# Slots stage of a fused transformer kernel: a second bank for turned context, weighing as a step's first work, softmax sums one step later with the product on Pool, other places for the layers

## The reference, cut to what matters

```
x_in = _ln(x, lnkv_g, lnkv_b);  k = x_in @ wk + bk;  v = x_in @ wv + bv
slots = q_mu + exp(q_logsig) * noise
for _ in range(3):
    prev = slots
    q = _ln(slots, lnq_g, lnq_b) @ wq + bq
    logits = einsum('bnd,bkd->bnk', k, q) / scale
    attn = softmax(logits, axis=-1) + 1e-8          # over the slots
    attn = attn / sum(attn, axis=1)                 # over the context rows
    upd = einsum('bnk,bnd->bkd', attn, v)
    slots = upd @ wu + bu + prev
    slots = gelu(_ln(slots, lnm_g, lnm_b) @ w1 + b1) @ w2 + b2 + slots
    slots = _ln(slots + x_cls[:, None, :], lnp_g, lnp_b)
```

## Time and profile before

| | us |
|---|---|
| median of 3 runs | 6898.41 (6891.54 to 6907.52) |
| profiled execution | 6899.85 |
| its span | 6897.9 |
| PE busy in the span | 6279.5 (91%) |
| starts of the first and the last score matmul (L3057) | 6233.5 and 6695.3 |
| POOL in the stage's steps | one instruction of 1.89 per step |

### The profile page before, as it was taken

One profiled execution on the slowest core, in us unless ns is written; L12 is line 12 of the kernel. 1 busy time (PEld: TensorE's weight loads), 2 busy tenths in 40 slices (PEclk: granted clock), 3 DMA queues, 4 the chain that ended last, 5 costly groups with the idle time before them and its releaser, 6 DMA issues.

```text
span 6897.9 us, 141178 instructions
## 1 busy us (share of the span) xinstructions
PE 6279.5 (91%) x56181; PEld 4521.0 (66%) x56181; DVE 3982.3 (58%) x8765; ACT 3322.4 (48%) x6373; POOL 2177.0 (32%) x2131
## 2 busy tenths in 40 slices
PE   5799999999999999999978899999699999998988
PEld 4466666666666666666645778777377777747873
DVE  2677777777777777777754244444444444354553
ACT  1466656656666566565643244444233333324543
POOL 3555555545555555555500000000011111082110
PEclk7899999999999999999987899999799999998778
DMA  1565656656656566565711000010100000030000
GB/s 45 90 106 88 105 91 101 107 87 99 100 94 105 89 100 105 87 101 97 114 37 29 19 25 30 28 36 10 34 10 13 11 14 14 18 99 1 1 1 22
DMA packets 396486, 407.87 MB, mean 59 GB/s; under 512 B 125575, under 2 KB 372946, under 8 KB 393786
## 3 DMA queue, kind: packets, MB, share of 16 engines
q1 hardware_dynamic: 395834, 398.85, 32.5%
HBM read 158.00 MB, written 0.46 MB: 23 GB/s over the span
## 4 chain that ended last, share of the span: by engine, by line
PE 75%; DVE 8%; ACT 5%; POOL 3%; issue 3%; DMA 2%; SPq 2%; DVEq 1%; POOLq 0%; ACTq 0%
PE psum L2205 9%; PE psum L2172 9%; PE psum L1546 6%; PE psum L1520 6%; PE psum L1534 6%; PE psum L2217 4%; PE psum L1560 4%; PE psum L1568 3%; PE psum L421 3%; PE psum L1666 3%; PE psum L435 3%; DVE row_max L1885 2%; PE psum L3057 2%; PE psum L1675 1%; DMA key_stack<-key_parts 1%
## 5 line engine op out<-in xcount | busy, mean ns | idle before, releaser
L1885 DVE TENSOR_REDUCE row_max<-psum 112x1 f32<-112x500 f32 x2304 | 1444.2, 668 | 291.8 <-PE psum L1534 287.1
L2003 ACT ACTIVATE weights<-psum 125x448 f32<-125x448 f32 x2304 | 1156.0, 544 | 783.8 <-PE psum L1520 769.0
L1520 PEld LDWEIGHTS psum<-query_stack,key_stack 121*125 121x125 bf16 x9216 | 839.2, 141 | 371.7 <-issue 171.3
L1534 PE MATMUL psum<-key_stack,query_stack 97*112 97x500 bf16 x2304 | 912.0, 397 | 102.0 <-DVE row_max L1885 76.8
L1520 PE MATMUL psum<-query_stack,key_stack 121*125 121x112 bf16 x9216 | 940.4, 226 | 70.1 <-ACT weights L2003 64.9
L2729 POOL TENSOR_TENSOR l_ctx_v<-l_ctx_v,l_ctx_w 125x512 f32<-125x512 f32 x48 | 60.9, 1270 | 2291.0 <-DVE l_ctx_v L2723 2291.0
L2205 PE MATMUL psum<-l_ctx_v,l_turned 125*128 125x128 f32 x5376 | 713.7, 281 | 16.0 <-ACT l_turned L2243 12.4
L2285 DVE TENSOR_REDUCE l_stat<-psum 128x1 f32<-128x1500 f32 (+1 forms) x224 | 391.5, 1748 | 577.3 <-PE psum L2172 577.3
L2205 PEld LDWEIGHTS psum<-l_ctx_v,l_turned 125*128 125x128 f32 x5376 | 643.1, 191 | 58.7 <-ACT l_turned L2243 40.1
L1546 PE MATMUL psum<-weights,values 125*17 125x112 f32 x18432 | 680.5, 266 | 0.2 <-ACT weights L2003 0.2
L1546 PEld LDWEIGHTS psum<-weights,values 125*17 125x17 f32 x18432 | 381.0, 98 | 265.3 <-ACT weights L2003 139.2
(11 more groups left out here) (526 smaller groups left out, 10421.3 us busy)
## 6 DMA issues: line engine op xcount, KB each, us to landing
key_stack<-key_parts SPq DMA_DIRECT2D x1728, 125.0 KB, 4.4
ctx_t<-in_ctxT SPq DMA_DIRECT2D x96, 750.0 KB
l_ctx_v<-in_ctxV SPq DMA_DIRECT2D x32, 750.0 KB
query_stack<-query_parts SPq DMA_DIRECT2D x576, 28.0 KB, 3.7
l_ctx_t<-in_ctxT SPq DMA_DIRECT2D x16, 750.0 KB
slot_context<-in_ctxV SPq DMA_DIRECT2D x16, 750.0 KB
key_stack<-ctx_mask_rows SPq DMA_DIRECT2D x576, 3.9 KB
sm_w<-in_sm_w SPq DMA_DIRECT2D x3, 2048.0 KB
```

Source lines behind the costliest of these rows:

```text
L1520: mm = e.matmul(self.k.psum[0:KN, h, (p % 4) * QC:(p % 4 + 1) * QC], ks[:, p, kt * KN:(kt + 1) * KN], q[:, p * QC:(p + 1) * QC])
L1534: e.matmul(self.k.psum[0:QC, 2 + n % 2, 0:500], q[0:ROWS_MAX, p * QC:(p + 1) * QC], ks[0:ROWS_MAX, p, c * 500:(c + 1) * 500]).then_inc(sel ...
L1885: e.tensor_reduce(self.largest[:, i % PAIRS, i // PAIRS:i // PAIRS + 1], k.psum[0:QC, 2 + i % 2, 0:500], AX.X, ALU.max, negate=True).then_ ...
L2003: e.activation(half(self.p[kt % 2], h), self.k.psum[0:KN, h, 0:HALF], ACT.Exp).then_inc(self.exped.sem, 1)
```

## The change

The turned thirds, joins and vu go round two banks, 5 and 7; what was in bank 7 (variance, spread, out, the second half of q) moves into columns 256 to 479 of bank 6, beside the first half. PE weighs step s-3 at place 0 (was s-2 at place 2), and scores at places 1 and 2 (were 0 and 1). DVE takes a step's softmax sums and reciprocals at the start of the step after (`sums_vector`); the product with them goes to POOL, ahead of its addition. DVE shifts at place 1 (was 0), ACT takes the exponential at place 2 (was 1) and copies the weighed rows at place 1 (was 2). ACT reads the centred values before it squares them, and makes the bias row of q that DVE made. The layers get new places.

```diff
-    ON_PE = {"vu": 1, "dev_m": 2, "var_m": 3, "rstd_m": 5, "h": 6, "out": 8, "dev_p": 9, "var_p": 10, "rstd_p": 12,
-             "dev_q": 13, "var_q": 14, "rstd_q": 16, "q": 17}
-    ON_ACT = {"dev_m": 2, "var_m": 3, "h": 6, "dev_p": 9, "var_p": 10, "affine": 13, "dev_q": 13, "var_q": 14, "q": 17}
-    ON_DVE = {"vu": 1, "around": 2, "var_m": 4, "rstd_m": 5, "out": 8, "var_p": 11, "rstd_p": 12, "add": 13, "var_q": 15,
-              "rstd_q": 16, "q": 17}
+    ON_PE = {"vu": 2, "dev_m": 5, "var_m": 6, "rstd_m": 7, "h": 8, "out": 9, "dev_p": 10, "var_p": 12, "rstd_p": 14,
+             "dev_q": 16, "var_q": 17, "rstd_q": 18, "q": 19}
+    ON_ACT = {"dev_m": 5, "var_m": 6, "h": 8, "dev_p": 10, "var_p": 12, "affine": 15, "dev_q": 16, "var_q": 17, "q": 19}
+    ON_DVE = {"vu": 2, "around": 3, "var_m": 6, "rstd_m": 7, "out": 9, "var_p": 12, "rstd_p": 14, "add": 15, "var_q": 17,
+              "rstd_q": 18, "q": 19}
...
-        self.turn = Banks(k, "slot_turn", [5], self.turn_order())
+        self.turn = Banks(k, "slot_turn", [5, 7], self.turn_order())
...
-                if late and p == 8 * (g - 1) + at - 13:
+                if late and p == 8 * (g - 1) + at - 16:
...
-        b6, b7 = k.psum[:, 6, 0:G], k.psum[:, 7, 0:G]
+        b6, b7 = k.psum[:, 6, 0:G], k.psum[:, 6, 256:256 + G]
...
-            if name == "var_m":
-                e.wait_ge(self.parts_ready.sem, self.parts_ready(min(u + 3, self.UNITS - 1)))
-            elif name == "var_q" and 0 < u < 4:
-                e.wait_ge(self.parts_ready.sem, self.parts_ready(u - 1))
...
-                if place < 2 and s < self.STEPS:
-                    self.score_tensor(e, s, place)
-                if place == 2 and 0 <= s - 2 < self.STEPS:
-                    self.weigh_tensor(e, s - 2)
+                if place == 0 and 0 <= s - 3 < self.STEPS:
+                    self.weigh_tensor(e, s - 3)
+                if place in (1, 2) and s < self.STEPS:
+                    self.score_tensor(e, s, place - 1)
...
+            e.activation(self.dev, b6, ACT.Identity, bias=shift)
             e.activation(self.sq, b6, ACT.Square, bias=shift).then_inc(self.sq_ready.sem, 1)
-            e.activation(self.dev, b6, ACT.Identity, bias=shift)
...
+            if u > 0:
+                e.wait_ge(self.parts_ready.sem, self.parts_ready(u - 1))
+            e.activation(self.c32, b7[0:96, :], ACT.Identity, bias=fcol[0:96, 8:9]).then_inc(self.row_ready.sem, 1)
...
-    def normalise_vector(self, e, n):
+    def sums_vector(self, e, n):
...
-        e.reciprocal(stat[:, 2, :], stat[:, 1, :])
-        e.drain()
-        e.tensor_tensor(a, a, spread(stat[:, 2, :], S), ALU.mult).then_inc(self.normed.sem, 1)
+        e.reciprocal(stat[:, 2, :], stat[:, 1, :]).then_inc(self.normed.sem, 1)
...
-            e.wait_ge(self.q_done.sem, self.q_done(u))
-            e.tensor_scalar(self.c32, b7[0:96, :], fcol[0:96, 8:9], None, ALU.add)
-            e.drain()
+            e.wait_ge(self.row_ready.sem, self.row_ready(u))
...
+            if 0 <= s - 2 < self.STEPS:
+                self.sums_vector(e, s - 2)
             if 0 <= s - 4 < self.STEPS:
                 self.join_vector(e, s - 4)
...
-                if place == 0 and 0 <= s - 1 < self.STEPS:
+                if place == 1 and 0 <= s - 1 < self.STEPS:
                     self.shift_vector(e, s - 1)
-            if 0 <= s - 1 < self.STEPS:
-                self.normalise_vector(e, s - 1)
...
             e.wait_ge(self.normed.sem, self.normed(n))
+            e.tensor_tensor(by_key, by_key, spread(self.stat[n % 3][:, 2, :], S), ALU.mult)
+            e.drain()
             e.tensor_scalar(a, a, 1e-8, None, ALU.add).then_inc(self.attn_ready.sem, 1)
```

More of the change, by code:

```diff
@@ L2953, in __init__ @@
         self.h_done, self.hid_ready, self.out_done = (sig(f"mlp_{n}", self.UNITS) for n in ("up", "act", "down"))
+        self.row_ready = sig("slot_row_ready", self.UNITS)
         self.z2_ready = sig("z_partly", self.UNITS)
@@ L3023, in fold_tensor @@
         else:
-            bk = k.psum[:, 7, :]
+            bk = k.psum[:, 6, :]
             e.wait_ge(self.fold_read.sem, self.fold_read(0))
@@ L3172, in side_scalar @@
     def side_scalar(self, e, name, u):
-        k, G, nth, col = self.k, self.G, self.nth, self.col
-        b6, b7 = k.psum[:, 6, 0:G], k.psum[:, 7, 0:G]
+        k, G, nth, col, fcol = self.k, self.G, self.nth, self.col, self.fcol
+        b6, b7 = k.psum[:, 6, 0:G], k.psum[:, 6, 256:256 + G]
         if name in ("dev_m", "dev_p", "dev_q"):
@@ L3211, in scalar @@
                     self.side_scalar(e, name, u)
[L3212 to L3219, removed]
+                if place == 1 and 0 <= s - 3 < self.STEPS:
+                    n = s - 3
                     e.wait_ge(self.weighed.sem, self.weighed(n))
@@ L3223, in scalar @@
                     e.activation(self.u_rows[n % 2], k.psum[:, 4, 0:129], ACT.Copy).then_inc(self.weighed_copied.sem, 1)
+                if place > 0 and self.turns(s + 1):
+                    self.turn_scalar(e, s + 1, place - 1)
+                if place == 2 and 0 <= s - 1 < self.STEPS:
+                    a = self.at[(s - 1) % 3][0:KN, 0:KT * S]
+                    e.wait_ge(self.shifted.sem, self.shifted(s - 1))
+                    e.activation(a, a, ACT.Exp, scale=float(np.sqrt(np.float32(D)))).then_inc(self.exped.sem, 1)
     def fold_vector(self, e, part):
@@ L3368, in gpsimd @@
             a = self.at[n % 3][0:KN, 0:KT * S]
+            by_key = a.rearrange("p (k s) -> p k s", s=S)
             e.wait_ge(self.normed.sem, self.normed(n))
+            e.tensor_tensor(by_key, by_key, spread(self.stat[n % 3][:, 2, :], S), ALU.mult)
+            e.drain()
             e.tensor_scalar(a, a, 1e-8, None, ALU.add).then_inc(self.attn_ready.sem, 1)
```

## The result

The changed kernel took 6762.75 us (6758.11 to 6767.43, 5 runs) against 6891.54 (6886.56 to 6907.52, 5 runs) of the kernel before beside it: a ratio of 0.9815, 95% interval 0.9802 to 0.9828, faster by 129 us. In a later series the same two stood at 6770.90 and 6873.37: 0.9845 (0.9829 to 0.9861), 102 us. The forecast was 6805, range 6773 to 6882: the direction and the likeliest case were right, the size too small, and the time lies 10 us under the range.

What follows compares the result with a forecast made beforehand. PE was taken as the bound, with gaps in which ACT decides. Work 326, gaps 5 + 5 + 2 and half clock 30 make 368 for 464; with the tail 94 less than 6899.85, so 6805, range 6773 to 6882.

Steps and rivals of the forecast that it cites:

- The p norm's two gaps: PE's waits of 0.91 and 0.89 us, for the p norm's reciprocal and before the query's centring; 9.9 us to go.
- POOL's pair: POOL's softmax product and addition: 3.6 us forecast; above 4.4 the weighing on PE would wait for it.
- The slower rival: PE waits at the weighing for POOL or late DVE sums, again a pair of gaps: 18 slower, 6917; 11%.
- The gaps only change places: ACT's order keeps thirds and joins waiting, a new pair replaces the p norm's: gain 0 to 20, about 6890; 9%.
- The clock keeps its mean: Falls come from the stage's matmuls, not gaps, so the clock stays 0.80: 44 us less in scoring, 6856; 25%.
- the matmul work of the 464 us: PE's busy 418.78 us while steps are scored, less half clock's cost: 418.78 - 186 + 93 = 326 us.
- The clock's 30: Cost in the scored stretch of 60 us at half clock instead of 186: the start and two or three short falls.
- the second bank's 5 us: What stays of turning steps' waits for ACT's copy (30.8 us before): 0.2 per step, 5 in all, ends 0 and 18.
- the m norm's 5: PE's wait for the m norm's reciprocal: 0.4 once per unit, taken as 0.5 each for 11 units, 5 us.
- the start's 2: ACT's later square delays var in steps 0 and 2, which have no weighing yet: about 1 us each.
- The tail's +2: After the last score, unit 10's m norm starts a step later, behind weighings: 2 us more, ends 0 and 5.
- a pair of gaps: Two PE waits of 0.91 and 0.89 us within 3 us, said to drop the clock to half for 20 us.

Runs made afterwards that it cites:

- gaps apart: Changed kernel with dead DVE instructions, three before the p norm's reciprocal and two before the m norm's, some 10 and 16 us apart: 6824.35 us.
- gaps at p: Changed kernel with three dead DVE instructions before the p norm's reciprocal and three before its product: 6825.70 us.

## Why the prediction was right and wrong

*Right.* PE's work plus gaps plus half clock was the sum to make, and the forecast's case came: the gaps went where it said, and the clock rose. The p norm's two gaps are gone; the m norm's is 0.36 for 0.4; no weighing waits for POOL but once for 0.3, behind the last score, and POOL's pair takes 3.36 with its drain, under the 4.4 from which it would have decided (forecast 3.6). The slower rival's wait is real: with the new places and the old weighing it was 18 to 19 us. "The gaps only change places" fell with the first waits. "The clock keeps its mean" fell too, 0.93 for 0.79.

*Wrong: the sizes of the sum.* It made 326 + 5 + 5 + 2 + 30 = 368 where 347.5 was measured. The step "the matmul work of the 464 us, run at full clock, is ... 326 us" was mis-sized by 9: it took the clock from a row with two digits, where 0.01 is 4.6 us, and a stretch 2 us longer; the measured work is 317 (320 in the kernel before, by the shorter stretch). The clock's 30 were 24. The gaps were 6.7 for 12: the second bank's 5 us were 0.3, the m norm's 5 were 2.2, the start's 2 were 0.9; one was not foreseen (the Gelu, 0.6 four times in steps with turning, where its table load stands behind the exponential's and a copy; a load is 1.28 in the earlier trace rows). So the score stretch gave 114.5 for 96: 7 by the work, 6 by the clock, 5 by the gaps. The tail's +2 was -3.9: it stood one step later, but at a clock of 0.75 instead of 0.61, which is 6 us less of half clock.

*Wrong: the base and the range.* From 6805 to 6762.75 are 42 us. 23 are the stage: its stretch and tail gave 118, the stage behind took 2 more, 117 for 94. 7 are the base: in that series the kernel before stood at 6891.5, not 6898.4, and 13 later runs of it have a median of 6873.37. The last 12 are scatter of whole times, which gave 129 once and 102 once around the stage's 117; the first block alone can account for such an amount. Take the stage's 117 from the recorded base, and the time is 6782, inside the range: it was base and scatter, not the stage, that took it out. The lower end was also mis-added: 326 without gaps and half clock is 138 less, and with 0 to 2 for the start and for the tail that is 6760 to 6764, not 6770; the range began higher still, at 6773. It left no room for scatter.

*The cause of a fall.* The prediction took a pair of gaps as the cause. The runs show that one gap of 1.3 can be enough for a short fall, that one of 2.1 to 2.2 brought 6.8 us each time in the kernel with gaps apart and up to 20 in the one with gaps at p, and that even 0.8 at times brings a long one. The prediction's own sign against itself was that the clock still falls once per unit with the pair gone. That came in part: it falls at four of the six m norms, behind 0.35 or 0.36, but for 3.4 us and not for 20. Most edits that added gaps added half clock, but two of the parts alone went the other way (new places, POOL's product), so the sum of the gaps is not what decides either; what does stays open. The prediction named a page that asks for a longer gap (the Trainium skill, TensorE: Matmul & The Clock Gate, section "Why this matters for your kernels"). These traces don't agree: the falls here stand behind gaps of 0.35 to 2.18 us.

## What to carry to other kernels

Where PE is the bound and its granted clock moves, split the stretch into work at full clock, gaps and the cost of half clock: the work is fixed, and over the whole change each microsecond of gap that went took about two of that cost with it, though not in every single edit. Which gap lowers the clock, and for how long, could not be told here, so measure the clock with each edit. Parts of an order written by hand need not add up: places, banks and POOL's product were worth 20, 50 and nothing that can be told alone, places and banks 54 together, and the whole 102 to 129; with the new places alone another wait showed, that of the weighing for POOL. Compare with a base run beside the change: medians of the kernel before went from 6898.41 (3 runs) over 6891.54, 6886.23 and 6880.67 to 6873.37 (13 runs) from series to series.

## What was not expected of the hardware

The dead DVE instructions have both inputs in SBUF. Three took 1.30 us where POOL stood still, and 2.44 where POOL worked (its product 6363.39 to 6364.70, its addition from 6364.86), in the kernel with gaps at p:

```profile
6363.88 2.44 DVE L3275 TENSOR_TENSOR slot_bias_rest<-slot_folded_w 96x224 f32<-96x224 f32 x3
...
6368.15 1.30 DVE L3275 TENSOR_TENSOR slot_bias_rest<-slot_folded_w 96x224 f32<-96x224 f32 x3
```

Of the 2.44 the first instruction, beside POOL's product, took 1.07 us, the second, at the head of POOL's addition, 0.82, and the third 0.39 as usual, though the addition still ran. In the kernel with gaps apart, two fell wholly into an addition and kept their length:

```profile
6275.96 0.84 DVE L3275 TENSOR_TENSOR slot_bias_rest<-slot_folded_w 96x224 f32<-96x224 f32 x2
```

```profile
6275.26 1.89 POOL L3377 TENSOR_SCALAR x_normed<-x_normed 125x672 f32<-125x672 f32 x1 [0.16 <-issue]
```

The Trainium skill, SBUF — State Buffer, section "Who interferes with whom", says that such an instruction and one of GpSimd's that reads SBUF contend, and that the one holds the other up wholly. This trace agrees beside POOL's product, but not behind the first 0.7 us or so of its addition. In the changed kernel two of DVE's instructions with SBUF inputs alone (L3284) fell beside POOL's addition, and kept their 0.45 us; none fell beside its product. So the change did not pay this price, by the order in which its work happened to fall.
